# A one-core decoder layer: start of the scan in another order, a bank of q ahead of the exponential, row gathers in waiting groups of eight

## The reference, cut to what matters

```python
x = x + mamba2(layernorm(x), W_in, conv_w, conv_b, dt_bias, A_log, D_param, norm_w, W_out)
x = x + cross_attention(layernorm(x), context, Wq, bq, Wk, bk, Wv, bv, Wo, qn_w, kn_w)
x = x + experts(layernorm(x), w_router, wg, wu, wd, sg, su, sd)

# mamba2: 64 heads of 64, state 128, one group
z, xBC, dt = split(h @ W_in.T)            # 4096, 4096 + 2 * 128, 64 columns
xs, B, C = split(silu(causal_conv4(xBC)))
dt = softplus(dt + dt_bias); dA = dt * -exp(A_log)
y[l] = sum over s <= l of (C[l] . B[s]) * exp(cumsum(dA)[l] - cumsum(dA)[s]) * dt[s] * xs[s] + D * xs[l]
out = rmsnorm(y * silu(z)) * norm_w @ W_out.T
# cross_attention: 16 query heads, 4 key heads of 128, 64 context tokens; q and k are RMS-normed, softmax(q k / sqrt(128)) v @ Wo
# experts: sigmoid router, the best 2 of 8 experts (width 640) per token, and 2 shared experts for all tokens
```

## Time and profile before

| | us |
|---|---|
| timed runs | 1716.67, 1717.10, 1723.58 |
| median | 1717.1 |
| the profiled execution, its own time | 1731.2 |
| its span in the profile | 1729.4 |
| TensorE busy | 1614.9 (93%) |
| VectorE, ScalarE, GpSimd busy | 1311.0, 1222.5, 601.3 |
| mean granted clock of TensorE | 0.973 of full speed |
| the scan, 128 rounds | from 97.6, its last products at 955.1 |

### The profile page before, as it was taken

One profiled execution on the slowest core, in us unless ns is written; L12 is line 12 of the kernel. 1 busy time (PEld: TensorE's weight loads), 2 busy tenths in 40 slices (PEclk: granted clock), 3 DMA queues, 4 the chain that ended last, 5 costly groups with the idle time before them and its releaser, 6 DMA issues. The chain is left out here.

```text
span 1729.4 us, 28895 instructions
## 1 busy us (share of the span) xinstructions
PE 1614.9 (93%) x9892; PEld 1289.2 (75%) x9892; DVE 1311.0 (76%) x2048; ACT 1222.5 (71%) x2531; POOL 601.3 (35%) x469
## 2 busy tenths in 40 slices
PE   4479999999999999999999999999968999999989
PEld 3257777777777777777777677777757889999868
DVE  7859999999999999999999756765557533333345
ACT  5669999999999999999999566665524333444321
POOL 1413343434343434343433321111112563336450
PEclk9679999999999999999999999999979999999989
DMA  8956444444444444444442100000132323222221
GB/s 309 393 212 246 162 155 170 148 163 154 170 149 162 155 170 150 169 147 171 148 170 98 55 1 1 1 1 1 47 105 84 127 103 110 93 91 96 79 86 43
DMA packets 74268, 220.30 MB, mean 127 GB/s; under 512 B 8848, under 2 KB 29584, under 8 KB 72464
## 3 DMA queue, kind: packets, MB, share of 16 engines
q1 hardware_dynamic: 68464, 192.38, 31.1%
q0 software_dynamic: 5664, 26.09, 4.3%
HBM read 184.62 MB, written 33.82 MB: 126 GB/s over the span
## 5 line engine op out<-in xcount | busy, mean ns | idle before, releaser
L607 POOL TENSOR_TENSOR m_gT<-m_gy,m_zs 128x512 f32<-128x512 f32 x128 | 166.7, 1302 | 537.5 <-DVE m_gy L769 537.5
L728 DVE SCALAR_TENSOR_TENSOR m_xc<-banks,k_cw,m_xc 128x510 f32<-128x510 f32 (+2 forms) x384 | 285.4, 743 | 21.1 <-ACT m_xc L647 12.1
L868 PE MATMUL m_ps_out<-k_won,m_gT 128*128 128x256 f32 x1024 | 242.3, 379 | 3.6 <-POOL m_gT L607 2.0
L825 PE MATMUL banks<-pair_hi,m_wxz 128*128 128x512 f32 x680 | 243.8, 409 | 0.5 <-DMA m_wxz<-w_split 0.5
L740 DVE TENSOR_TENSOR m_mat<-m_mat,k_cbm 128x768 f32<-128x768 f32 x256 | 232.5, 950 | 2.0 <-ACT m_mat L668 2.0
L868 PEld LDWEIGHTS m_ps_out<-k_won,m_gT 128*128 128x128 f32 x1024 | 193.6, 189 | 36.6 <-POOL m_gT L607 3.3
L856 PE MATMUL m_ps_y<-m_mat,m_xdt 128*64 128x256 f32 (+1 forms) x2048 | 194.7, 332 | 0.0
L668 ACT ACTIVATE m_mat<-m_mat 128x1536 f32<-128x1536 f32 x128 | 188.5, 1473 | 0.1
L856 PEld LDWEIGHTS m_ps_y<-m_mat,m_xdt 128*64 128x64 f32 x2048 | 126.8, 136 | 80.0 <-issue 42.3
L659 ACT ACTIVATE m_mat<-m_a_all,k_cum 128x256 f32<-128x256 f32 x340 | 170.7, 502 | 0.0
L618 POOL TENSOR_TENSOR m_g_sum<-m_g_sum,m_g_sq 128x512 f32<-128x512 f32 x124 | 163.2, 1316 | 5.2 <-ACT m_g_sq L674 5.1
(11 more groups left out here) (305 smaller groups left out, 3695.9 us busy)
## 6 DMA issues: line engine op xcount, KB each, us to landing
m_wxz<-w_split SPq DMA_DIRECT2D x85, 512.0 KB, 3.3
m_a_all<-a_by_head SPq DMA_DIRECT2D x85, 512.0 KB, 4.3
k_w_first<-w_split SPq DMA_DIRECT2D x43, 512.0 KB, 3.4
k_a_first<-a_by_head SPq DMA_DIRECT2D x43, 512.0 KB, 4.3
w_split<-p_w_hl SPq DMA_DIRECT2D x16, 1024.0 KB, 9.9
raw<-in_w_gate_up POOLq DMA_DIRECT2D x9, 1280.0 KB, 6.8
raw<-in_w_xz SPq DMA_DIRECT2D x16, 512.0 KB, 7.9
raw<-in_w_down POOLq DMA_DIRECT2D x9, 640.0 KB, 7.9
```

Source lines behind the costliest of these rows:

```text
L607: pool.tensor_tensor(gT[:, n % 2, :], gy[:, n % 2, :], zs[:, n % 2, :], ALU.mult).then_inc(g_done, 1)
L728: dve.scalar_tensor_tensor(out=out[:, :, k:], in0=ps[:, :, 0:SEQ - k], scalar=cw[:, c, TAPS - 1 - k:TAPS - k], in1=out[:, :, k:], op0=ALU. ...
L825: last = pe.matmul(ps[:, :], w, a, start=m == 0, stop=m == len(terms) - 1)
L868: last = pe.matmul(ps_out[:, q * HID:(q + 1) * HID], gT[:, n % 2, q * P:(q + 1) * P], won[:, c, :], start=c == 0 and q % 2 == 0, stop=c == ...
```

## The change

Preparation: the buffers of the split weights are taken in the order 0, 1, 3, 2, and piece 15 is split into the raw buffer instead of a slot of `w_hl` (`hl`, `last_hl`). Its `w_high` no longer waits for a store but for GpSimd's subtraction of piece 13, and stands at the end of ScalarE's list; that of piece 14 stands one step earlier. The semaphores `w_stored` outlive the block: its end waits for the stores of pieces 12 and 13 only, those of 14 and 15 are waited for in the scan, by GpSimd ahead of its first product and by SyncE at round 8. The four transfers to `a_dram` are spread over pieces 8 to 11. `w_low(0)` and `w_low(1)` stand inside VectorE's norm loop.

Scan: `z_proj(0)` comes before `x_proj(1)`; ScalarE's and VectorE's lists ahead of the loop are in another order, with `scale_x(1)`, `tanh_x(1)`, `tanh_z(1)` and the gaps of round 2 drawn ahead of the loop.

Attention: `q_out(b+1, 2)` stands before `exp(b, 0)`.

Experts: GpSimd waits, after each four tiles of gathers, for their landing, and the list `COMBINED` says which tiles VectorE combines at steps 4 to 19 of dense(1): tiles 0 to 3 as before, none at step 8, tiles 4 to 13 one step later, tiles 14 and 15 both at step 19.

```diff
--- before.py
+++ after.py
@@ -47,7 +47,7 @@
     xT_hi, xT_lo, cbm, dt, cum, cw, cb, d_ch, won, neg_half, ones, a_dram, w_dram = kept
-    w_first, a_first, w_first_loaded, a_first_loaded = first
+    w_first, a_first, w_first_loaded, a_first_loaded, w_stored = first
     NCT = w_xz.shape[1]
@@ -103,6 +103,7 @@
         w_hl = sb("w_hl", [P, RING, CH, 2, XZ], F32R)
+        last_hl = raw[:, 0:2 * CH * XZ].bitcast(F32R).rearrange("p (c s m) -> p c s m", c=CH, s=2)
@@ -114,7 +115,7 @@
             sem(n) for n in ("wdt_loaded", "wbc_loaded", "small_loaded", "wo_loaded"))
-        w_loaded, w_stored = ([sem(f"{n}{u}") for u in range(RING)] for n in ("w_loaded", "w_stored"))
+        w_loaded = [sem(f"w_loaded{u}") for u in range(RING)]
         w_hi_done, w_lo_dve, w_lo_pool, a_stored = (
@@ -140,6 +141,11 @@
+        def hl(j):
+            if j == NJ - 1:
+                return last_hl
+            return w_hl[:, (0, 1, 3, 2)[j % RING]]
+
         def wait_low(eng, j):
@@ -174,15 +180,15 @@
                 sp.dma_start(w_dram[j * CH:(j + 1) * CH].rearrange("c p m -> p c m"),
-                             w_hl[:, j % RING].rearrange("p c s m -> p c (s m)").bitcast(F32))\
+                             hl(j).rearrange("p c s m -> p c (s m)").bitcast(F32))\
                     .then_inc(w_stored[j % RING], 16)
...
                         .then_inc(w_first_loaded, 16)
-                if j == NJ - 6:
+                if NJ - 8 <= j < NJ - 4:
                     sp.wait_ge(aT_done, 2)
-                    for q in range(TPG):
+                    for q in (j - NJ + 8,):
                         r, i = q // 2, q % 2
@@ -192,8 +198,10 @@
                         .then_inc(a_first_loaded, 16)
-            for u in range(RING):
-                sp.wait_ge(w_stored[u], 16 * len(range(u, NJ, RING)))
+            sp.wait_ge(w_stored[0], 16 * (NJ // RING))
+            sp.wait_ge(w_stored[1], 16 * (NJ // RING))
+            sp.wait_ge(w_stored[2], 16 * (NJ // RING - 1))
+            sp.wait_ge(w_stored[3], 16 * (NJ // RING - 1))
@@ -223,8 +231,8 @@
                 pool.wait_ge(w_hi_done, j + 1)
-                pool.tensor_tensor(w_hl[:, j % RING, :, 1, :], w_raw[:, j % RING],
-                                   w_hl[:, j % RING, :, 0, :].bitcast(F32), ALU.subtract).then_inc(w_lo_pool, 1)
+                pool.tensor_tensor(hl(j)[:, :, 1, :], w_raw[:, j % RING], hl(j)[:, :, 0, :].bitcast(F32), ALU.subtract)\
+                    .then_inc(w_lo_pool, 1)
@@ -242,9 +250,11 @@
                 act.wait_ge(w_loaded[j % RING], 16 * (j // RING + 1))
-                if j >= RING:
+                if j == NJ - 1:
+                    act.wait_ge(w_lo_pool, NJ - 2 - LOW)
+                elif j >= RING:
                     act.wait_ge(w_stored[j % RING], 16 * (j // RING))
-                act.activation(w_hl[:, j % RING, :, 0, :], w_raw[:, j % RING], ACT.Copy).then_inc(w_hi_done, 1)
+                act.activation(hl(j)[:, :, 0, :], w_raw[:, j % RING], ACT.Copy).then_inc(w_hi_done, 1)
@@ -304,8 +314,11 @@
                 tanh(m)
-                if m + 9 < NJ:
+                if m + 9 < NJ - 2:
                     w_high(m + 9)
+                elif m == NM - 2:
+                    w_high(NJ - 2)
+            w_high(NJ - 1)
@@ -322,8 +335,8 @@
                 dve.wait_ge(w_hi_done, j + 1)
-                dve.tensor_tensor(w_hl[:, j % RING, :, 1, :], w_raw[:, j % RING],
-                                  w_hl[:, j % RING, :, 0, :].bitcast(F32), ALU.subtract).then_inc(w_lo_dve, 1)
+                dve.tensor_tensor(hl(j)[:, :, 1, :], w_raw[:, j % RING], hl(j)[:, :, 0, :].bitcast(F32), ALU.subtract)\
+                    .then_inc(w_lo_dve, 1)
@@ -341,14 +354,16 @@
                     xT_low(n - 2)
+                if n == 11:
+                    w_low(0)
+                if n == NT - 1:
+                    w_low(1)
             xT_low(NT - 2)
...
             dve.tensor_scalar(cb[:], cb[:], 0.5, None, ALU.mult).then_inc(halved, 1)
-            w_low(0)
-            w_low(1)
             dve.wait_ge(dt_exp, 1)
@@ -593,6 +608,8 @@
                 if n == 8:
+                    sp.wait_ge(w_stored[2], 16 * (NCT // 8))
+                    sp.wait_ge(w_stored[3], 16 * (NCT // 8))
                     for dst, src, loaded in next_loads:
@@ -624,6 +641,7 @@
+            pool.wait_ge(w_stored[2], 16 * (NCT // 8))
             for n in range(N):
@@ -692,14 +710,21 @@
             scale_x(0)
-            for n in range(2):
-                gaps(n, 0)
-                gaps(n, 1)
-                decays(n)
-                if n == 0:
-                    tanh_x(0)
-                    tanh_z(0)
-            for n in range(N):
+            gaps(0, 0)
+            gaps(0, 1)
+            tanh_x(0)
+            decays(0)
+            tanh_z(0)
+            scale_x(1)
+            gaps(1, 0)
+            gaps(1, 1)
+            tanh_x(1)
+            decays(1)
+            tanh_z(1)
+            gaps(2, 0)
+            gaps(2, 1)
+            decays(2)
+            for n in range(1, N):
                 if n + 1 < N:
@@ -783,8 +808,8 @@
             conv_x(0)
+            silu_x(0)
             matrices(0)
-            silu_x(0)
             silu_z(0)
@@ -892,8 +917,8 @@
             x_proj(0)
+            z_proj(0)
             x_proj(1)
-            z_proj(0)
             for n in range(N):
@@ -933,7 +958,8 @@
         first = (sb("w_first", [P, 2, 2, KK, P], F32R)[:], sb("a_first", [P, 2, TG])[:],
-                 ctx.enter_context(nc.semaphore("w_first_loaded")), ctx.enter_context(nc.semaphore("a_first_loaded")))
+                 ctx.enter_context(nc.semaphore("w_first_loaded")), ctx.enter_context(nc.semaphore("a_first_loaded")),
+                 [ctx.enter_context(nc.semaphore(f"w_stored{u}")) for u in range(4)])
         retired = mamba_prepare(nc, xres, ident, raw, banks, scratch, kept, first, x, w_xz, w_bc, w_dt, conv_w, conv_b, dt_bias, a_log,
@@ -1206,9 +1232,9 @@
                     q_out(b + 1, 1)
+                    q_out(b + 1, 2)
                 exp(b, 0)
                 if more:
-                    q_out(b + 1, 2)
                     q_out(b + 1, 3)
@@ -1652,6 +1678,7 @@
     UNIT_READY = [TPG, 2 * TPG + LATE, 3 * TPG + LATE, NT]
+    COMBINED = [*([t] for t in range(TPG)), [], *([t] for t in range(TPG, NT - 2)), [NT - 2, NT - 1]]
     TURN = {2: TPG + LATE, 3: TPG + LATE + 2, 7: 2 * TPG + LATE, 8: 2 * TPG + LATE + 2, 12: 3 * TPG + LATE}
@@ -1849,6 +1876,8 @@
             for n in range(NT):
+                if n and n % TPG == 0:
+                    pool.wait_ge(gathered[n // TPG - 1], 16 * TOP * TPG)
                 if n >= NT // TOP:
@@ -2151,7 +2180,8 @@
                         if d == 1 and k >= HT - NT:
-                            combine(k - HT + NT)
+                            for t in COMBINED[k - HT + NT]:
+                                combine(t)
                     if u == UNITS - 1:
```

## The result

The changed kernel takes 1702.55 us (median of four runs, 1701.35 to 1704.55). The forecast was 1703.5, within 1695 to 1710. The kernel before took 1717.83 beside it (four runs, 1716.67 to 1723.58); the ratio is 0.9902, with a 95% interval of 0.9885 to 0.9918, so 14 to 20 us less by the interval.

A forecast was written before the change was run, and what follows sets the result against it. TensorE, busy 93%, was taken to bound most of the kernel, transfers the preparation, ScalarE the scan's start-up. Gains of 5.9, 7.7 and 0 us took the timed median from 1717.1 to 1703.5, range 1695 to 1710 (forecast's own 1701 to 1707).

The forecast's parts named there:

- the bounds of the two parts: Ranges of gain: preparation and start of the scan 3.5 to 7 us, attention's third bank of q 3 to 8.
- part 3: Last dense pass: gathers in waiting groups, combines one step later; claimed 0, at most +0.9 us, timed runs having next to no pauses.
- Part 1, hand-over: Preparation to scan: waiting only for the stores of pieces 12 and 13 starts the scan at 91.4, 6.2 us earlier.
- Part 1, start-up order: Start of the scan: ScalarE bounds it, the new order saves nothing by itself; late weights cost 0.9 us, 0.6 covered.
- The landing order of transfers: Start of the scan: transfers land in queue order, round 1's weights behind two stores at 98.3; otherwise the 0.9 us would go.
- Part 2: Attention: third bank of q emptied before the exponential removes TensorE's waits in seven batches, 7.7 us less.
- the rival: Attention: it only moves its wait, to the softmax or the fifth bank, yielding under 3 us; total 1708.5, chance 0.10.
- The rival that named the mechanism: Last dense pass: pauses are in the timed runs and grouping shrinks them, 8 us more; total 1695.5, chance 0.13.
- waits breed pauses: Rival at the gathers: a longer stream of groups that each follow a landing adds 21.6 us; total 1725, chance 0.05.
- The cover of the combines: Last dense pass: at step 8 `combine(4)` would want its rows 0.9 us too soon; the empty slot buys that cover.

The follow-up runs named there:

- whole_again: The changed kernel, unaltered, run again beside the kernel before on a later chip: 1702.70 us for 1729.87, ratio 0.9839.
- old_start: The changed kernel with the scan's lists ahead of its loop back in their old order on TensorE, ScalarE and VectorE: 1707.32 us, ratio 0.9872.
- before_again: The kernel before, unaltered, run once more for its profile beside its timed runs: 1732.08 us beside 1730.08.
- p3_alone: The kernel before with only the gathers' waits in groups of eight and the new list of combines: 1720.08 us for 1731.01, ratio 0.9938.
- waits_only: The changed kernel with the combines in their old order, keeping the grouped gathers and their waits: 1704.79 us, ratio 0.9843.
- p12: The changed kernel without the gathers' waits and the new order of the combines: 1715.15 us for 1731.01, ratio 0.9914.
- p1_alone: The changed kernel with attention, gathers and combines as before, keeping only preparation and start of the scan: 1724.07 us for 1731.01, ratio 0.9962.

## Why the prediction was right, and where it was not

**The time.** 1717.1 - 13.6 = 1703.5 against 1702.55. The terms were 5.9, 7.7 and 0. In the result's own runs the 15.3 measured fits 7.4, 7.7 and nearly nothing, but no part was measured alone beside them. Where the whole change ran again it gave 27.2 (`whole_again`), beside 7.4 + 7.7 + 11.3 = 26.4 by the table, the last term being 105.1 (mean of the six kernels without waits among the gathers) less 93.8 (mean of the five with three waits and the new combines, groups of eight). That the forecast time came out is in part luck: it was reckoned from the one set of timed runs in which before seems to be free of the pauses. From before's 1729.87 beside `whole_again`, 13.6 us less would have been 1716.3, and 1702.70 was measured. The range was also tighter than its own terms: the bounds of the two parts (3.5 to 7, 3 to 8) and 0 to 0.9 for part 3 add up to 1702.1 to 1711.5, not to 1701 to 1707.

**Part 1, hand-over: right, under-sized.** Forecast 91.4, came at 89.2 to 90.5, mean 89.8; the old one at 97.3 to 97.7. Stores of piece 13 landed at 89.3 where I had 90.9. I reckoned back from the landing of piece 14 and took nothing for the first stores' earlier entry, which the rows from 25 us on show in the changed kernel (DMA share 0.90, 1.02 and 0.60; before 0.46, 0.69 and 1.02):

```profile
25.00:30.00 5.00, 3.55 (x22) 2.60 (x22) 4.37 (x12) 3.67 (x8) 0.00 (x0) 1.00 0.90 365
30.00:35.00 5.00, 5.00 (x31) 4.37 (x31) 2.36 (x3) 1.69 (x3) 0.00 (x0) 1.00 1.02 417
35.00:40.00 5.00, 3.42 (x15) 2.44 (x13) 4.86 (x6) 4.68 (x7) 0.00 (x0) 1.00 0.60 161
```

The transfers run full from 30 us on, and part of that lead is lost again from 35 to 40 us. That the rest is what made 89.3 of 90.9 was not tested by itself.

**Part 1, start-up order: the step that failed.** "The new order holds the same instructions, so it saves nothing by itself": it saves 5.1 us (`old_start`), more than two thirds of part 1. I took ScalarE's unbroken work from 100.53 to 116.84 as the bound and charged the late weights of round 1 with 0.9 us. But they land at 97.2 (I had 98.3), and with the old lists `tanh_z(0)` inherits them, through `z_proj(0)` behind `x_proj(1)`. The cost of an order has to be read with the new arrival times, not with those of before, under which the same order did no harm. The errors partly cancel in the sum: 5.9 forecast, 7.4 measured. That it came so near is luck: `old_start`, which the account valued within 1 us of the changed kernel, keeps only 2.3 of the 7.4.

**The landing order of transfers.** The second projection's weights land at 97.25 behind stores 14 and 15, and at 94.36 when store 15 stands behind them: they seem to keep their place in the queue. By the Trainium skill (DMA: Bandwidth & Descriptors, Queues, rings and completion order) each DMA engine works a ring's descriptors in order; these two rows agree, though a queue that shared its time among the transfers would also be quicker with one store fewer.

**Part 2: right in mechanism and size.** 7.7 forecast, 7.7 measured; batches of 31.4 for 32.6 as forecast; the `exp` starts without idle time, and the transposes 0.06 us behind their input, the near miss on which the rival stood.

**Part 3: wrong where the pauses are present.** "The timed runs have next to none of these pauses, and then the grouping has nothing to remove" rested on one difference of 14.1 us between one profiled execution and three timed ones. It held for those timed runs, as far as can be told. On the three chips of the later runs before took 1724 to 1735 us in all of its 51 runs (the ten of `before_again` among them), and each profile with long rows of gathers that was taken there has the pause. The rival that named the mechanism (pauses in the timed runs, shrunk by grouping) had 0.13 and priced it at 8 us; it is 11.3. What I held against it, that ScalarE's pause at the grouped scatters is the longer one, is a length of idle time, not of the path: it cost 3.7 us against 12.2. Of the 13.40 us, some 8.1 are no pause at all: ScalarE stands idle 8.08 us at the same place in the changed kernel, where no signal is late. That waits breed pauses is excluded by the 93.4 us pass of `p3_alone`.

Beside that, the Trainium skill (Runtime: NRT & Kernel Launch, The ~15µs preamble/postamble breakdown) puts 6.2 us between a profile's total and the reported time. The runs here don't give that total, only the span from first to last instruction. Every run that lists a span shows 1.7 to 1.8 us from it to the time (1701.57 for 1699.8), the profiled ones like the others, so the 14.1 us lay between executions and nothing is to be taken off for the profile; the measurement decides.

**The cover of the combines: not shown.** GpSimd idles 2.0 to 2.2 us at the three group ends (forecast 1.7), and no VectorE wait for the gathers was seen in the changed kernel. But none was seen with the old order in `waits_only` either, so the 0.9 us that the empty step was to save was not there to be saved in that run. The passes of 93.0 and 94.6 us don't price it: the difference is TensorE's clock ahead of the first gather.

**Open.** What holds TensorE's signals up while GpSimd issues indirect transfers is not shown. The trace names no source, and whether it is the issuing, the transfers in flight or their number was not taken apart. Which chip the result was measured on is not on record, so whether the chip makes the difference between before's 1717 there and 1730 in the later runs, or something that changed with time, is open. It fits pauses that come in some sets of runs and not in all, but no profile of a run at 1717 was seen; a stretch at another clock, as below, could be part of it.

## What to carry to other kernels

When a profiled execution is longer than the timed runs, the difference may be a stall that other sets of runs have every time: price the removal both ways and keep both in the range, as large cases, not small ones. Long rows of indirect transfers beside a dense pass are worth breaking with a wait for landing about every ten microseconds, if what they feed has the slack: at the gathers it gave 11 us where signals came late, at the scatters a wait more every 5 us cost 9. When a start is moved ahead, write out every engine's list again with the new arrival times; the item that used to come first may now be the one that all the others stand behind. And before the idle time ahead of a late start is called a pause, look up when the work it waited for was done: of 10.50 us of idle time here, 1.9 were late.

## What was not expected of the hardware

TensorE's signals came up to 12.9 us late (in `p12`; 12.7 in before) while GpSimd issued indirect transfers in rows, 1.25 us each. No late signal of ScalarE or VectorE was found at the gathers. It happens with rows of eight too, at the scatters above all, where it mostly costs little. But `p1_alone` shows that it can cost more there, and that a wait for landing does not always end it: an up product ended at 1353.89, GpSimd waited for the landing of its eight scatters until 1355.8, and VectorE's `h` was released at 1364.65, 10.8 us late; the stretch took 67.4 us for the usual 61 to 62. With rows of four no late signal was seen in the one profile there is.

The first stretch of the experts' phase, the same products in every kernel, took 38.8 to 38.9 us in six profiles and 41.9 to 43.7 in the eight others: all four with the old part 1, and four of the ten with the new. Whether the change has a hand in that is open. In before and in the changed kernel the granted clock tells the two apart; TensorE had stood idle for 1.7 of the 5 us ahead of the one pair of rows and for 2.2 ahead of the other, so its work just before does not tell them apart. Before, then after:

```profile
1285.00:1290.00 5.00, 4.04 (x12) 3.12 (x12) 2.28 (x6) 1.63 (x4) 0.91 (x1) 0.68 1.05 350
1290.00:1295.00 5.00, 3.96 (x23) 3.30 (x22) 2.96 (x7) 2.22 (x5) 0.00 (x0) 0.84 1.05 349
```

```profile
1273.00:1278.00 5.00, 3.59 (x18) 2.82 (x18) 2.51 (x7) 2.32 (x6) 0.23 (x1) 1.00 1.04 349
1278.00:1283.00 5.00, 5.00 (x29) 4.33 (x30) 2.71 (x7) 2.96 (x5) 0.00 (x0) 1.00 1.04 348
```

This alone moves single profiles of one kernel by 3 to 5 us, which is why the parts are read here from stages over many kernels and not from one pair of spans.
